# Transformer layer with routed experts on one core: scatters, shared pairs and products in another order, POOL for four final sums

## The reference

```python
mod = silu(c) @ wmod                                  # 6 vectors for each of 8 batches: sa, ca, ga, sb, cb, gb
h = layernorm(x) * (1 + ca) + sa
x = x + ga * attention(h)                             # 32 heads of 8, window of 8, then a projection
h = layernorm(x) * (1 + cb) + sb                      # 2048 tokens of 256
scores = sigmoid(h @ gate_w.T); topv, topi = top_k(scores, 2); topv /= topv.sum()
y = mlp(h, sw1, sw2, sw3)                             # shared expert, 352 hidden
for e in range(16):                                   # routed experts, 176 hidden
    y += mlp(h, w1[e], w2[e], w3[e]) * weight_of(e)   # zero unless e is one of a token's two
return x + gb * y                                     # mlp(x) = (silu(x w1') * (x w3')) w2'
```

## Time and profile before

| what | us |
|---|---|
| median of 3 runs | 410.24 (409.18 to 412.09) |
| the profiled execution | 408.21 |
| its span in the trace | 406.4 |

### The profile page before, as it was taken

How to read it: one execution, slowest core, us unless ns; L and a number is a source line. 1 busy time by engine, 2 the same in 40 slices (tenths; PEclk the granted TensorE clock), 3 DMA queues, 4 the chain that set the end, 5 groups by cost and what they waited for, 6 DMA issues and landing times.

```text
span 406.4 us, 12935 instructions
## 1 busy us (share of the span) xinstructions
PE 357.5 (88%) x5187; PEld 266.9 (66%) x5187; DVE 284.5 (70%) x632; ACT 157.3 (39%) x374; POOL 120.9 (30%) x149
## 2 busy tenths in 40 slices
PE   7876988999998999878768696699999999998994
PEld 4555877888787787766535264477777777774463
DVE  2758496979788898999833623568777777761597
ACT  1142253544545463401323100345555555551440
POOL 6300004040404030121587173034343444442000
PEclk9999899999999999988995989879999999999999
DMA  8736355564646343424252023123333333201943
GB/s 278 223 92 179 91 135 147 148 182 115 177 104 186 93 147 92 145 83 144 57 206 104 26 104 106 54 79 117 118 113 118 113 116 82 68 10 59 316 143 103
DMA packets 56124, 50.55 MB, mean 124 GB/s; under 512 B 22768, under 2 KB 50841, under 8 KB 55938
## 3 DMA queue, kind: packets, MB, share of 16 engines
q1 hardware_dynamic: 43360, 30.17, 26.0%
q10 hardware_dynamic: 8914, 11.13, 8.8%
q0 software_dynamic: 3792, 8.43, 5.9%
HBM read 28.70 MB, written 20.87 MB: 122 GB/s over the span
## 4 chain that ended last, share of the span: by engine, by line
PE 70%; DVE 15%; issue 6%; DMA 3%; POOL 2%; ACT 2%; ACTq 1%; SPq 0%; DVEq 0%; POOLq 0%
PE bank L1508 11%; PE bank L1523 11%; PE bank L1384 8%; PE bank L1337 6%; PE bank L1272 6%; PE bank L1464 6%; PE bank L1310 3%; PE bank L1319 3%; PE bank L1291 3%; PE bank L1516 3%; PE bank L1491 3%; PE bank L1352 2%; DMA first_region<-wmod 2%; DVE region L870 2%; PE bank L1330 2%
## 5 line engine op out<-in xcount | busy, mean ns | idle before, releaser
L555 POOL DMA_INDIRECT yrows<-second_region,sloti x47 | 46.2, 984 | 77.6 <-ACT second_region L760 76.0
L1384 PE MATMUL bank<-xT_region,sw 128*128 128x512 f32 (+1 forms) x96 | 48.2, 655 | 3.8 <-DVE second_region L998 3.8
L1523 PE MATMUL bank<-w,second_region 88*128 x188 | 50.3, 391 | 1.2 <-DVE second_region L1135 1.2
L1508 PE MATMUL bank<-first_region,second_region 128*128 x141 | 43.4, 317 | 3.4 <-DVE second_region L1125 2.2
L1508 PE MATMUL bank<-region,second_region 128*128 x141 | 43.3, 316 | 0.0
L522 POOL DMA_INDIRECT hslots<-hxw,posi x32 | 31.7, 992 | 32.1 <-DVE posi L989 23.2
L1337 PE MATMUL bank<-region 128*32 128x16 f32 x2048 | 35.3, 212 | 3.1 <-issue 3.1
L1337 PEld LDWEIGHTS bank<-region 128*32 128x32 f32 x2048 | 35.1, 159 | 3.4 <-issue 3.4
L499 POOL TENSOR_TENSOR rstd2s<-ve,cft 128x2 f32<-128x2 f32 x8 | 5.7, 708 | 105.2 <-DVE ve L919 105.1
L1384 PEld LDWEIGHTS bank<-xT_region,sw 128*128 128x128 f32 (+1 forms) x96 | 18.5, 198 | 27.8 <-issue 22.2
L1523 PEld LDWEIGHTS bank<-w,second_region 88*128 88x128 f32 x188 | 33.1, 196 | 4.6 <-issue 1.7
(11 more groups left out here) (169 smaller groups left out, 683.0 us busy)
## 6 DMA issues: line engine op xcount, KB each, us to landing
region<-hslots SPq DMA_DIRECT2D x47, 129.0 KB
hslots<-zeros ACTq DMA_DIRECT2D x8, 516.0 KB
region<-vd SPq DMA_DIRECT2D x64, 64.0 KB, 2.2
region<-yrows SPq DMA_DIRECT2D x16, 256.0 KB, 6.0
modb<-moddram SPq DMA_DIRECT2D x8, 384.0 KB, 4.1
xs<-x SPq DMA_DIRECT2D x8, 256.0 KB, 3.9
vd<-second_region SPq DMA_DIRECT2D x8, 256.0 KB, 2.9
out<-xs SPq DMA_DIRECT2D x8, 256.0 KB, 2.1
```

Of the source, the lines that this page charges most:

```text
L555: gp.indirect_dma_start(yrows, bass.IndirectOffsetOnAxis(ap=sloti[:, s:s + 1], axis=0), yo[:, s % RING, :], None, bounds_check=TOPK * T - ...
L1384: last = pe.matmul(o[0:p], sw13[:, c, half * SI + f * P:half * SI + f * P + p], xT[:, c, g * GT * P:(g + 1) * GT * P], start=c == 0, stop= ...
L1508: last = pe.matmul(UP(s), parts[:, s % 2, m, c * P:(c + 1) * P], w13[c][:, bass.ds(experts[s], 1), :], start=m == c == 0, stop=m == EXACT ...
L1523: last = pe.matmul(YP(s), hT2[0:IH, s % 2, k, :], w2[:, k, bass.ds(experts[s], 1), :], start=k == 0, stop=k == 1)
```

## The change

- `EARLY` is (4, 5): scatters 5 to 8 of round 0 move behind `rstd2(7)`. Scatter 13 waits until pair 3 is through PE (`REST`).
- PE does `count(1)` ahead of the first half of pair 4. DVE does `times_b(3)` ahead of `ranked(1)`.
- `yo` changes places with the tiles' buffers, which no longer overlap those of the pairs. Pairs 6 and 7 (`EXTRA = 2`) are done ahead of the routed tiles on PE, ACT and DVE; the first turned tile waits for the product of pair 6, the first `up` for that of pair 7.
- DVE does `goes_to` of tiles 0 to 3 ahead of `less_high(0)`.
- `finish` of batches 0 to 3 is done by POOL (`BY_POOL = 4`), behind its last `give`, with a semaphore of its own.
- The order of the silus and products at the end follows from that.

```diff
@@ -61,6 +61,10 @@
 
 PIECE = 1024
 PIECES = ((), (0, 1), (2, 3), (4, 5), (6, 7), (8, 9), (10,), ())
+
+BY_POOL = 4
+
+EXTRA = 2
 
 AHEAD = 2
 NONE = 8192
@@ -217,6 +221,8 @@
         sloti = sb("sloti", [P, NS], I32)
         expert = sb("expert", [P, NS + 2], I32)
 
+        last.at = late.at
+        yo = last.take("j d", (RING, D,))
         at_rows = (TOPK * TT + GT * AHEAD) * D
         rows = region[:, at_rows:at_rows + RING * RW].rearrange("p (j d) -> p j d", d=RW)
         parts = last.take("j m t", (2, EXACT, C * P,), BF16)
@@ -224,9 +230,6 @@
         act_s = last.take("j w", (2, I,))
         hid = last.take("j w", (2, I,))
         hT2 = last.take("j k t", (2, 2, P,))
-
-        last.at = late.at
-        yo = last.take("j d", (RING, D,))
 
 
 
@@ -322,7 +325,7 @@
         fetch = [sem(f"fetch{k}") for k in range(RING)]
         put = [sem(f"put{k}") for k in range(RING)]
         ld_y = [sem(f"ld_y{k}") for k in range(B)]
-        f_a, f_b, f_c, f_d, f_e = (sem("f_" + n) for n in "abcde")
+        f_a, f_b, f_c, f_d, f_p = (sem("f_" + n) for n in "abcdp")
 
         ld_c, ld_cf, ld_qkv, ld_cb, ld_wp = (sem("ld_" + n) for n in ("c", "cf", "qkv", "cb", "wp"))
         warm_s = sem("warm_s")
@@ -456,7 +459,10 @@
                     sp.dma_start(yk[:, k, U * b:U * b + U, :], y_t[b, :, TOPK - 1 - k]).then_inc(ld_y[b], 16)
             out_t = out.rearrange("(b u p) d -> b p u d", u=U, p=P)
             for b in range(B):
-                sp.wait_ge(f_d, b + 1)
+                if b < BY_POOL:
+                    sp.wait_ge(f_p, b + 1)
+                else:
+                    sp.wait_ge(f_d, b - BY_POOL + 1)
                 sp.dma_start(out_t[b], xs[:, U * b:U * b + U, :]).then_inc(st_out, 16)
             sp.wait_ge(st_out, 16 * B)
 
@@ -538,12 +544,16 @@
                         place_rows(0, i)
 
 
-            EARLY = (4, 9)
+            EARLY = (4, 5)
+
+            REST = 13
             rstd1(0)
             rstd1(1)
             over(main)
             rstd2(B - 1)
             for i in range(EARLY[1], TOPK * ROUND[1]):
+                if i == REST:
+                    gp.wait_ge(su_p, 4)
                 place_rows(0, i)
             for i in range(TOPK * (ROUND[2] - ROUND[1])):
                 place_rows(1, i)
@@ -558,6 +568,15 @@
 
             for s in range(NS):
                 give(s)
+
+            def finish(b):
+                gp.wait_ge(f_c, b + 1)
+                gp.wait_ge(sh_s, min(U * b + U, GT * AHEAD))
+                v = xs[:, U * b:U * b + U, :]
+                gp.tensor_tensor(v, v, yk[:, 0, U * b:U * b + U, :], ALU.add).then_inc(f_p, 1)
+
+            for b in range(BY_POOL):
+                finish(b)
 
 
         @block.scalar
@@ -737,7 +756,7 @@
             gate_exp(B - 2)
             turned_h(B - 1)
             gate_exp(B - 1)
-            for n in range(2, SK * AHEAD):
+            for n in range(2, SK * AHEAD + EXTRA):
                 silu_g(n)
 
             def silu(s):
@@ -778,7 +797,6 @@
                 if s + 4 < NS:
                     high(s + 4)
             result(NS - 1)
-            silu_g(SK * AHEAD)
 
             def scaled_y(b):
                 act.wait_ge(ld_y[b], 16 * TOPK)
@@ -789,17 +807,16 @@
                                           scale=gatew[:, 0, U * b + u:U * b + u + 1])
                 last.then_inc(f_a, 1)
 
-            silu_g(7)
             silu_g(8)
             scaled_y(0)
+            silu_g(9)
             scaled_y(1)
-            silu_g(9)
             scaled_y(2)
+            silu_g(10)
             scaled_y(3)
-            silu_g(10)
             scaled_y(4)
+            silu_g(11)
             scaled_y(5)
-            silu_g(11)
             scaled_y(6)
             scaled_y(7)
 
@@ -1101,10 +1118,10 @@
             pick(1, 1)
             chosen(1)
             times_b(2)
+            times_b(3)
             ranked(1)
             new_tiles(1)
             placed(1)
-            times_b(3)
             behinds()
             times_b(4)
             times_b(5)
@@ -1113,6 +1130,8 @@
             owned()
             for t in range(GT, GT * AHEAD):
                 keep_shared(t)
+            for n in range(EXTRA):
+                times_b(SK * AHEAD + n)
             gates()
 
             def less_high(s):
@@ -1134,6 +1153,8 @@
                 wait(dve, y_p, s - 1)
                 dve.tensor_copy(hT2[0:IH, s % 2], HT(s)).then_inc(ht_s, 1)
 
+            for s in range(RING):
+                goes_to(s)
             less_high(0)
             less_high(1)
             low(0)
@@ -1143,8 +1164,6 @@
             low(2)
             less_high(3)
             hidden(1)
-            for s in range(4):
-                goes_to(s)
             for s in range(NS):
                 turned_hidden(s)
                 if s + 3 < NS:
@@ -1185,26 +1204,20 @@
                 v = xs[:, U * b:U * b + U, :]
                 dve.tensor_tensor(v, v, yk[:, 0, U * b:U * b + U, :], ALU.add).then_inc(f_d, 1)
 
-            times_b(6)
-            times_b(7)
+            times_b(8)
             for k in range(RING):
                 dve.wait_ge(put[k], 16 * len(range(k, NS, RING)))
-            times_b(8)
             combine(0)
             modulated_y(0)
-            finish(0)
             times_b(9)
             combine(1)
             modulated_y(1)
-            finish(1)
+            times_b(10)
             combine(2)
-            times_b(10)
             modulated_y(2)
-            finish(2)
             combine(3)
             times_b(11)
             modulated_y(3)
-            finish(3)
             combine(4)
             combine(5)
             with_shared(8)
@@ -1473,9 +1486,8 @@
             up_half(2, 1)
             gate(B - 1)
             up_shared(3)
-            up_half(4, 0)
             count(1)
-            up_half(4, 1)
+            up_shared(4)
             up_shared(5)
             pe.wait_ge(lg_s, B)
             pe.wait_ge(rank_s, ROUNDS)
@@ -1524,7 +1536,9 @@
                                      start=k == 0, stop=k == 1)
                 last.then_inc(y_p, 1)
 
-            pe.wait_ge(su_m, SK * AHEAD)
+            for n in range(EXTRA):
+                up_shared(SK * AHEAD + n)
+            pe.wait_ge(su_m, SK * AHEAD + EXTRA - 1)
             pe.wait_ge(ld_ew, 16 * FIRST_PARTS)
             pe.wait_ge(ld_late, 16)
             pe.wait_ge(wide_s, 11)
@@ -1532,6 +1546,7 @@
             turn_rows(0)
             load_experts(0)
             turn_rows(1)
+            pe.wait_ge(su_m, SK * AHEAD + EXTRA)
             up(0)
             turn_rows(2)
             up(1)
@@ -1548,7 +1563,7 @@
                     pe.wait_ge(sya_s, GT * AHEAD)
                 down(s)
 
-            for n in range(SK * AHEAD, SK * GROUPS):
+            for n in range(SK * AHEAD + EXTRA, SK * GROUPS):
                 up_shared(n)
             pe.wait_ge(yo_s, NS)
             for g in range(AHEAD, GROUPS):
```

## The result

The changed kernel takes 396.51 us (median of 4 runs, 392.69 to 399.13) where the kernel before takes 411.16 (median of 4): a ratio of 0.960, 95% interval 0.949 to 0.972. Every ratio here goes by each kernel's fast runs alone (those within 1.5% of its fastest), so it need not be the quotient of the medians of all runs. The profiled executions are 395.91 and 408.21 us, their spans 394.1 and 406.4. In the last series of experiments the same two kernels came out at 415.62 and 411.02: ratio 1.010, interval 1.005 to 1.015. That series ran on another chip than the two series before it (chips 13, 15 and 6 in the record, which doesn't name the chip of this first pair). "After" is always the first profile of the changed kernel; "after2" is the one of the last series.

The account below looks back on a forecast made before the run. PE, 88% busy, was taken as the bound on average, with POOL's scatters holding up the routing and half clock following PE's idling. Front 10.1 plus tail 4.0 makes 14.1 us off 410.24: 396.0 us, range 391 to 402.

Parts of the forecast that it names:

- the front: Routing up to the start of the tiles: gain 9.2 us if PE is early, 11.1 if late; 10.1 taken.
- the tail: Work behind the tiles: 6.2 us gained, less 2.2 for POOL's adds blocking DVE, gives 4.0; bounds 1.0 and 6.2.
- PE early: Ahead of the tiles: PE's strand 1.7 us before the loads, idles about 4 us, half clock stays; gain 7.5 + 1.7 = 9.2.
- a case that didn't come: Ahead of the tiles: PE's strand 2.2 us behind the loads, hardly idles, no half clock; gain 5.8 + 5.3 = 11.1.
- Scatters behind `rstd2(7)`: Second half of routing: `rstd2(7)` 4.13 us earlier at 205.85, PE idle 0.5 us, no first half-clock spell, `chances(1)` at 214.2.
- Routing: `chances(1)` to last scatter: `ranked(1)` at 220.0, positions at 224.2, rest of 0.3 us, last scatter ends at 241.1.
- PE's strand: PE ahead of the tiles: `down_shared` takes 10.4 to 14.3 us, pairs 6 and 7 end at 243.6 to 247.5.
- PE's strand becomes the bound: Rival, front: a 10 us half-clock spell within 219 to 243 costs 5.1; first product 255.3, total 404.0 us; chance 0.10.
- slower: Rival: half clock over the whole front, first product at about 274, 18.6 us late; total 419.5 us; chance 0.03.
- Start of the tiles: First products: first at 248.4 to 250.1, a gain of 7.5 to 5.8 us; the 1.7 us fifth-load wait goes.
- the term of 3.6 for the clock: First to sixth product: of 5.3 us lost, 3.6 is half clock, which stays if PE is early.
- The stores: End of kernel: stores of batches 0 to 3 waiting for POOL cost nothing, covered by about 3 us.

Follow-up runs that it names:

- early49: The changed kernel with scatters 5 to 8 back ahead of `rstd2(7)` (`EARLY = (4, 9)`): 404.22 us, ratio 0.988 to the kernel before.
- the third series: Last set of runs, on another chip: changed kernel again 415.62 us (ratio 1.010), kernel before 411.02, a version joining helpful edits 412.91, old order around `count(1)` 413.57.
- warm: The changed kernel plus 36 small matmuls into unused PSUM that keep PE busy ahead of the tiles: 394.16 us, ratio 0.963 to the kernel before.
- norest: The changed kernel without scatter 13's wait for pair 3 (`REST = -1`): 395.88 us, ratio 0.965 to the kernel before.
- bypool0: The changed kernel with all eight `finish` sums on DVE, each right behind its product (`BY_POOL = 0`): 395.82 us, ratio 0.968 to the kernel before.

## Why the prediction held, step by step

It said 396.0 and the front 10.1, the tail 4.0 us. The profiled pair gives 10.0 and 2.3, 12.3 in all (408.21 to 395.91). The medians differ by 14.7, so 2.4 us are the distance of the profiled executions from their medians: the total fits better than its terms. The front's 10.0 are 6.9 at the first product and 3.5 from there to the sixth, less 0.4 behind it. For the case that came, PE early, my sum had 9.2; that 10.1 was hit comes from taking the mean with a case that didn't come, and is luck.

- *Scatters behind `rstd2(7)`:* as worked out. 206.16 for 205.85, PE idle 0.92 us for 0.5, no spell, `chances(1)` 214.37 for 214.2. `early49` loses 7.1 us without the move, up to 2.3 of them by the rest.
- *Routing:* `ranked(1)` 219.97 for 220.0, positions out at 224.20 for 224.2, last scatter out at 241.69 for 241.1; idle ahead of the resting one 0.42 us where 0.30 is usual.
- *PE's strand:* `down_shared` took 10.7 us, the low end of 10.4 to 14.3, and pairs 6 and 7 ended at 244.0. That the lower end came rested on signals that arrive at once. The rival "PE's strand becomes the bound" had the right place and the wrong cause: in the third series this strand is late by 19 us by waits, 16.71 of it in one. I had the 3.9 us by which `down_shared` was longer in before as a bound, and didn't ask what they were. This is the step that fails in the third series. Late signals were in no rival; "slower" had a delay of that size, 18.6 us, from half clock alone, and its 0.03 was worked out for that cause only.
- *Start of the tiles:* the first product at 248.95 (248.4 to 250.1), no wait for the fifth load. PE was early and idled 4.1 us as foreseen, and a spell came, but of 3 us instead of 6.45. So the term of 3.6 for the clock was too large for this case: without the spell the start is 1.3 us shorter (`warm`).
- *Tail:* 2.3 for 4.0. The part that was argued from the earlier trace rows is right in size: 0.15 + 1.01 + 1.00 = 2.2 us of longer `combine`, forecast 2.2. Mis-sized were the waits, 0.69 + 0.39 for ACT behind the loads and 0.53 + 0.51 for PE at half clock, 2.1 us where I had 0.5 (`norest` and `warm`, without that spell, end 1.9 us sooner); the start, `combine(0)` 8.64 us after the tiles instead of 7.7; and the other way DVE's work of 19.4 for 20.0. Together 0.9 + 1.6 - 0.6 = 1.9 less, against 1.7 measured.
- The stores cost nothing, as forecast: the span ends 2.6 us after DVE in both profiles.

The Trainium skill ("SBUF — State Buffer", "Who interferes with whom") spoke against POOL's sums, and the traces agree with it in direction: `combine` is 2.2 us longer in all. With `bypool0` at 395.82 the sums are no gain.

## What to carry to other kernels

Read from which instruction a small gap comes before counting it as slack or as bound: a few us of waiting for matmuls that had long been done were the trace of an effect that grew to 17 us in the third series, where the scatters ran without a break. Scatters queued ahead of a short operation that others wait for were paid in full, and moving them was worth more than the pairs, the sums and the rest together. And kernels related to the changed one held their gain on two chips and lost it on a third: time both kernels on more than one chip, and more than once, before believing 4%.

## What was not expected of the hardware

- Signals from PE to ACT and DVE were up to 17.5 us late, 10 us and more into an unbroken row of indirect DMAs of 1.265 us each, with the records of those DMAs incomplete (119 for 512 increments). Other kernels with such a row had every signal within 0.02 us.
- POOL's sum of 128x512 that reads SBUF and DVE's two-input `combine` lengthen each other: 1.89 for 0.88 us and 2.24 for 1.27. A memset of the same size, 0.52 us, leaves DVE at 0.87.
- After idling 3.3 to 3.6 us, half clock lasted 10.25 us in one kernel and 3 in another; with three idles of 1.58, 1.06 and 1.46 us it came too, for 3 us.
